# First attention of a four-layer stack: column sums in groups of four, turned scores issued earlier, the last softmax moved ahead of band products

## The reference

```python
def _L0_attn_ref(x, w_qkv, w_out, pos_bias, scale_embed, if_gain):
    _OFFSETS = list(range(41)) + [128, 48, 192]
    qkv = x @ w_qkv
    q, k, v = jnp.split(qkv, 3, axis=-1)        # then (B, H, T, HD)
    idx = jnp.arange(T)[:, None] - deltas[None, :]
    valid = idx >= 0
    k_g = k[:, :, idxc]
    v_g = v[:, :, idxc]
    k_mod = k_g * (1.0 + scale_embed)
    scores = jnp.einsum('bhtd,bhtjd->bhtj', q, k_mod) * scale
    scores = scores + pos_bias.T[None, :, None, :]
    scores = jnp.where(valid[None, None], scores, jnp.finfo(scores.dtype).min)
    attn = jax.nn.softmax(scores, axis=-1)
    out = jnp.einsum('bhtj,bhtjd->bhtd', attn, v_g)
    out = out * if_gain[None, :, None, None]
    return out @ w_out

x = x + 0.5 * _L0_ffn_ref(_layernorm(x), ...)
x = x + _L0_attn_ref(_layernorm(x), ...)
x = x + 0.5 * _L0_ffn_ref(_layernorm(x), ...)
```

## Time and profile before

| | |
|---|---|
| median of three runs | 3477.29 us (3476.79 to 3479.61) |
| the profiled execution, its own time | 3482.6 us |
| its span | 3480.8 us |
| busy: PE, DVE, ACT, POOL | 89%, 70%, 52%, 25% |
| the attention stage's products, first to last sum | 121.7 to 363.5 us |
| last `close` of the stage (L787) | 429.5 us |

### The profile page before, as it was taken

One profiled execution on the slowest core, in us unless ns is written; L12 is line 12 of the kernel. 1 busy time (PEld: TensorE's weight loads), 2 busy tenths in 40 slices (PEclk: granted clock), 3 DMA queues, 4 the chain that ended last, 5 costly groups with the idle time before them and its releaser, 6 DMA issues. The chain is left out here.

```text
span 3480.8 us, 62786 instructions
## 1 busy us (share of the span) xinstructions
PE 3111.7 (89%) x24941; PEld 1708.0 (49%) x24941; DVE 2437.7 (70%) x5433; ACT 1804.4 (52%) x3292; POOL 857.5 (25%) x801
## 2 busy tenths in 40 slices
PE   4899868999799999999798979888998899898899
PEld 3455745666522222222465557566776223332677
DVE  8877388778599999994877854645335888883433
ACT  2222236777467777777577753133222366677221
POOL 0324109677200000000867720001302111212000
PEclk9899979999879999999999989898999599998899
DMA  1044403111150000000311110001101400000100
GB/s 53 14 123 120 98 9 83 27 35 31 44 187 1 2 1 1 2 1 1 80 29 35 32 35 1 2 27 49 49 1 58 124 2 30 34 2 1 47 1 13
DMA packets 77882, 129.26 MB, mean 37 GB/s; under 512 B 12772, under 2 KB 52616, under 8 KB 77384
## 3 DMA queue, kind: packets, MB, share of 16 engines
q1 hardware_dynamic: 77592, 125.25, 12.7%
HBM read 77.39 MB, written 34.19 MB: 32 GB/s over the span
## 5 line engine op out<-in xcount | busy, mean ns | idle before, releaser
L2008 ACT ACTIVATE AR<-ps 128x1024 f32<-128x1024 f32 (+2 forms) x756 | 717.6, 995 | 289.4 <-PE ps L1909 220.8
L2091 DVE TENSOR_REDUCE AR<-ps 128x1 f32<-128x512 f32 x1296 | 809.2, 683 | 48.1 <-PE ps L1878 47.1
L1909 PE MATMUL ps<-AR 32*128 32x512 bf16 (+3 forms) x4992 | 537.9, 378 | 9.3 <-ACT AR L2008 5.6
L1878 PE MATMUL ps<-AR 32*128 32x512 bf16 (+3 forms) x1664 | 478.3, 397 | 43.8 <-DVE AR L2091 13.4
L1926 PE MATMUL ps<-AR 128*32 128x512 f32 (+3 forms) x3328 | 439.1, 601 | 4.3 <-ACT AR L2013 3.9
L2500 PEld LDWEIGHTS ps<-AR 128*128 128x128 f32 x3072 | 362.9, 192 | 60.5 <-issue 47.5
L1878 PEld LDWEIGHTS ps<-AR 32*128 32x128 bf16 x1664 | 119.7, 92 | 551.1 <-DVE AR L2091 411.1
L2659 DVE SCALAR_TENSOR_TENSOR X<-ps,AR,X 128x128 f32<-128x128 f32 x512 | 143.7, 344 | 345.7 <-PE ps L2500 345.3
L2500 PE MATMUL ps<-AR 128*128 128x128 f32 x3072 | 363.1, 275 | 0.0
L2475 PE MATMUL ps<-XT,AR 128*128 128x512 f32 x672 | 307.7, 594 | 0.0
L1909 PEld LDWEIGHTS ps<-AR 32*128 32x128 bf16 x4992 | 185.1, 94 | 152.8 <-ACT AR L2008 48.2
(11 more groups left out here) (326 smaller groups left out, 5150.5 us busy)
## 6 DMA issues: line engine op xcount, KB each, us to landing
AR<-AR SPq DMA_DIRECT2D x124, 128.0 KB, 2.3
band<-AR SPq DMA_DIRECT2D x32, 450.0 KB, 4.7
AR<-band SPq DMA_DIRECT2D x32, 448.0 KB, 5.0
AR<-in_c_rot SPq DMA_DIRECT2D x64, 128.0 KB, 2.2
AR<-in_L3f_w SPq DMA_DIRECT2D x30, 256.0 KB, 5.7
rows_KA<-AR SPq DMA_DIRECT2D x32, 128.0 KB, 2.4
AR<-scr_bias SPq DMA_DIRECT2D x32, 128.0 KB, 3.2
AR<-in_L2f_w SPq DMA_DIRECT2D x30, 128.0 KB, 2.7
```

The lines of the kernel that those rows point to most:

```text
L1878: e.matmul(g.bank[b][:, 0:w], QA[rows, q, 128 * i:128 * i + 128], KA[rows, q, 512 * first:512 * first + w], start=way != "kept", stop=True ...
L1909: t = e.matmul(g.bank[h][:, lo:512], K[32 * h:32 * h + 32, q, 128 * kt:128 * kt + 128], Q[32 * h:32 * h + 32, q, queries], start=y == 0, s ...
L2008: e.activation(dst[:, :, lo:512], src[:, :, lo:512], ACT.Exp, scale=self.scale).then_inc(*s.up("exp" if u else "left", k, i, *((1,) if u e ...
L2091: e.tensor_reduce(o, g.bank[b][:, 0:w], AXX, ALU.max).then_inc(*s.up("reduced", k, n, h, st, kc))
```

## The change

`scores` gives each step its place itself. Where the plan before had one `gather` between two products, four products behind, it now has four gathers in a row after every fourth product, the last of the four being two products behind. `lift` is split: `raise` is PE's part (L634), placed ahead of DVE's part, which keeps the name. For the first three chunks it stands at the place of the `exp` of the tile before. In the last chunk the lift, exp and norm steps of the four tiles stand close together, ahead of most band products of the third chunk (tiles 10 and 11), and every `through` of the last chunk stands ahead of the next tile's first turn. The `close` of chunk 2 moves to directly behind the third chunk's last tile and takes the statistics of the next stage's chunks 0 to 2 with it. In `sync` the loads 12 to 14 move behind the store of the next tile, and POOL's three first roots move ahead. The same work is done as before.

```diff
--- before.py
+++ after.py
@@ -471,7 +471,7 @@
 
 
 
-    SCORE_LAG, NPR, FAR, ROW, KEYS = 4, 11, (41, 43), 1800, 112
+    NPR, FAR, ROW, KEYS = 11, (41, 43), 1800, 112
 
     def allocate(self, g):
         ar = g.ar
@@ -502,29 +502,31 @@
         self.WO = ar.f32(4, 128)
         at = []
         for c in range(4):
-            at += [(c + (i + 0.5) / (2 * NJ), x) for i, x in enumerate(self.scores(c))]
+            at += self.scores(c)
             at += [(0.1 + 0.1 * b, ("project", 0, 0, b)) for b in range(8) if not c]
             for i in range(4):
-                soft = c + 1.02 + 0.15 * i
-                at += [(soft, ("lift", c, i, 4 * c + i)), (soft + 0.05, ("exp", c, i, 4 * c + i)),
-                       (soft + 0.12, ("norm", c, i, 4 * c + i))]
-                far = soft + 0.67
-                at += [(far + 0.02 * y, ("turn", c, y, 4 * c + i)) for y in range(4)]
-                at += [(far + 0.1, ("value", c, i, 4 * c + i)), (far + 0.13, ("taken", c, i, 4 * c + i)),
-                       (far + 0.16, ("through", c, i, 4 * c + i))]
-            at += [(far + (0.36 if c == 2 else 0.18), ("close", c, 0, 0))]
+                n = 4 * c + i
+                soft = c + 1.04 + 0.15 * i if c < 3 else 4.03 + 0.03 * i
+                norm = soft + (0.12 if c < 3 else 0.04)
+                at += [(soft - (0.09 if i and c < 3 else 0.02), ("raise", c, i, n)), (soft, ("lift", c, i, n)),
+                       (soft + (0.05 if c < 3 else 0.01), ("exp", c, i, n)), (norm, ("norm", c, i, n))]
+                far = soft + 0.67 if c < 3 else 4.3 + 0.2 * i
+                at += [(far + 0.02 * y, ("turn", c, y, n)) for y in range(4)]
+                at += [(far + 0.1, ("value", c, i, n)), (far + 0.13, ("taken", c, i, n)), (far + 0.16, ("through", c, i, n))]
+            at += [(far + 0.18, ("close", c, 0, 0))]
         self.plan = [x for _, x in sorted(at, key=lambda y: y[0])]
 
     def scores(self, c):
+
         js = []
         for gr in range(6):
             js += [j for j in [8 * gr + x for x in (0, 2, 4, 6, 1, 3, 5, 7)] if j < NJ]
         out = []
-        for i in range(NJ + self.SCORE_LAG):
+        for i in range(NJ + 2):
             if i < NJ:
-                out.append(("product", c, js[i], NJ * c + i))
-            if i >= self.SCORE_LAG:
-                out.append(("gather", c, js[i - self.SCORE_LAG], NJ * c + i - self.SCORE_LAG))
+                out.append((c + (i + 0.5) / NJ, ("product", c, js[i], NJ * c + i)))
+            if i % 4 == 1 and i > 4:
+                out += [(c + min(i + 0.5, NJ - 0.1) / NJ, ("gather", c, js[y], NJ * c + y)) for y in range(i - 5, i - 1)]
         return out
 
     def by_pool(self, n):
@@ -552,14 +554,12 @@
         wo = I["L0_attn_w_out"].rearrange("(g a d) n -> a d g n", g=4, a=4, d=8)
         for a in range(4):
             e.dma_start(self.WO[32 * a:32 * a + 8, :, :], wo[a]).then_inc(*s.up("d_w2", k, a, by=16))
-        for x in range(14):
+        for x in range(16):
             self.store(e, s, x)
-            if x < 13:
+            if x < 12:
                 self.load(e, s, x)
-        self.load(e, s, 13)
-        self.store(e, s, 14)
-        self.store(e, s, 15)
-        self.load(e, s, 14)
+            if x > 12:
+                self.load(e, s, x - 1)
         self.load(e, s, 15)
 
     def store(self, e, s, x):
@@ -620,7 +620,7 @@
                     e.wait_ge(*s.at("s8", k, *((c, gr - 2) if gr > 1 else (c - 1, gr + 4))))
                 e.matmul(g.bank[b][p:p + 32, :], self.W2[:, j, :], self.PR[n % self.NPR], start=j % 2 == 0,
                          stop=j % 2 == 1, skip_group_check=True).then_inc(*s.up("gathered", k, n))
-            if what == "lift":
+            if what == "raise":
                 if j == 0:
                     e.wait_ge(*s.at("s8", k, c, 5))
                 if n:
@@ -780,13 +780,11 @@
                                 ALU.mult).then_inc(*s.up("weighted", k, n, "run"))
                 e.tensor_tensor(to[:, :, 48], self.SM[:, j, :, 42], self.sm[:, j, :], ALU.mult).then_inc(*s.up("weighted", k, n))
             if what == "close":
-                for i in range(3) if c == 3 else ():
-                    settle(e, s, g, k + 1, i)
                 xs = g.X[:, 4 * c:4 * c + 4, :].rearrange("p a b -> p (a b)")
                 e.wait_ge(*s.at("through", k, 4 * c + 3))
                 e.tensor_tensor(xs, g.bank[7], xs, ALU.add).then_inc(*s.up("added", k, c))
-                if c == 3:
-                    settle(e, s, g, k + 1, 3)
+                for i in range(3) if c == 2 else (3,) if c == 3 else ():
+                    settle(e, s, g, k + 1, i)
 
     def gpsimd(self, e, s):
         g, k = self.g, self.k
@@ -832,8 +830,10 @@
                 e.tensor_tensor(self.UF, far, bc(self.WF[:, n % 4, 1, :], [128, 16, 8], 2), ALU.mult).then_inc(*s.up("unit", k, n, 1))
                 e.wait_ge(*s.at("unit", k, n, 1))
                 e.tensor_tensor(to, to, self.UF, ALU.add).then_inc(*s.up("paired", k, n))
-        for c in range(4):
-            root(e, s, g, k + 1, c)
+            if what == "value" and n == 13:
+                for i in range(3):
+                    root(e, s, g, k + 1, i)
+        root(e, s, g, k + 1, 3)
 
 
 class Timetable:
```

## The result

| | before | after |
|---|---|---|
| median of the runs on the same chip | 3478.45 us (3476.79 to 3483.91, 4 runs) | 3456.2 us (3452.05 to 3457.85, 4 runs) |
| ratio to before, 95% | 1 | 0.9932 [0.9914, 0.9949] |
| the profiled execution, its own time | 3482.6 us | 3454.95 us |
| its span | 3480.8 us | 3453.2 us |
| first product of the stage, last `close` | 121.75, 429.54 us | 120.79, 409.42 us |

The change saves 22.3 us by the medians, 0.7%. The forecast was 3460 (3445 to 3472), faster by over 0.2%.

A forecast was written before the change was run, and what follows sets the result against it. The stage was taken to alternate: DVE sets the pace in chunk 0 and each later chunk's first half, PE in the second half and tail. Terms 5 - 6.1 - 9.7 - 10.1 + 0.5 + 3 = -17.4 gave 3460 us (3445 to 3472).

The forecast's parts named there:

- Chunk 0, +5: First chunk: DVE waits longer for V projections standing directly behind a group of sums; +5 us, bounds 0 and 8.
- Chunk 1, -6.1: First lift to lift of tile 4: 58.4 us in place of 64.5, with 16 products' sums in four blocks.
- Chunks 2 and 3, -9.7 and -10.1: Lone sums between turns merge: 61.4 us for 71.15 and 60.4 for 70.5, including DVE waits of 2.7 and 1.5.
- The tail, +0.5: Lift of tile 12 to last close: 61.7 us against 61.2, as the new order adds waits; bounds -3 and +6.
- the clock, +3: Granted clock falls behind PE waits at three places, tail and middle of chunks 2 and 3; 3 us together, 0 to 8.
- the 4.4 us wait: In the tail PE stands 4.4 us at tile 10's projection, its values' copy queued on ACT behind three exponentials.
- The sum, -17.4: Whole kernel: 5 - 6.1 - 9.7 - 10.1 + 0.5 + 3 = -17.4 us, giving 3460 us.
- Waits at tiles 4, 8 and 12: Sign of being right: DVE's waits for PE's turned scores at these tiles fall to about 8 to 12 us.
- The busy time of L621 near 70 us: Sign of being right: PE's busy time for the sums falls from 116 us towards 70.
- Groups that give it back: Rival, 8%: groups stop PE until their last product, keeping chunks 2 and 3 at 70 us; kernel 3477.
- The slower case: Rival, 6%: repeated waits keep the tail's clock at its lower level, last five tiles +34 us; kernel 3491.
- Fuller overlap: Rival, 6%: DVE's waits vanish, chunks 2 and 3 take about 51 us each, not 61; kernel 3440.

The follow-up runs named there:

- e1: Kernel before with the groups of four sums alone, turned scores directly ahead of the lift, last chunk in its old order: 3474.25 us, ratio 0.9983.
- e6: Changed kernel with the eight V projections of chunk 0 placed just ahead of a group of sums instead of behind it: 3446.45 us, ratio 0.9907.
- e8: Changed kernel with V projections ahead of groups, last chunk's output projections behind the next first turn, second tile's exponential earlier, closes of chunks 0 and 1 later: 3439.33 us.
- e4: Kernel before with the last chunk's new order, close, loads and roots alone: 3477.96 us, ratio 0.9994.
- e9: Changed kernel with band products of the first three chunks 0.50 instead of 0.67 of a chunk behind their softmax: 3466.84 us, ratio 0.9963.

## Why the prediction was right

The time lies in the range and the mechanism holds, with one reservation that e1 shows (chunks 2 and 3 below). Three sums were loose: the waits listed for chunk 0 add up to 5.8 rather than 5, and six tiles of band products at the prices given are 39.6 us rather than 40.2, and the upper bounds reach 21.3 us rather than 22. None changes the forecast by more than 1 us.

**Chunk 0, +5.** Measured +4.3, which is just the change in these waits (5.60 less 1.32). The waits of L745 are as named: 1.94 at the start (1.32 before), 1.02 at projection 3, 1.62 at 5 (forecast 1.5) and 1.02 at 6 (1.0); those expected at 4 and 7 did not come. e6 shows that they are the cause, and that the term could have been had at less than nothing.

**Chunk 1, -6.1.** Measured -5.0. The granted clock was 0.83 in this chunk against 0.92 before: turned scores at 166.37 us took 5.52, as they had before the change, and those at 187.43 did so again, behind waits of 2.16 and 0.73 us for products. The second fall is new (5.45 us from start to start in place of 2.97) and is more than the missing 1.1 us; how much of it reached the end of the chunk was not separated. The clock's price stood in a term of its own, but that term had expected falls in chunks 2 and 3 and not here.

**Chunks 2 and 3, -9.7 and -10.1.** Measured -10.0 and -10.3. The steps hold one by one: waits of 2.34 and 1.53 us for the exponential and the `close` where 2.7 and 1.5 were worked out, lone sums that merge at 1.0 for a block. One block of each chunk costs 1.82 instead of 1.0, which the sum had missed. What the words ahead of it left out is that the merging gives this only together with the earlier turned scores: the sum used both (it let no lift inside a chunk wait), the sentence named one. e1 alone is 5.1 us in chunk 3.

**The tail, +0.5, and the clock, +3.** The tail measured +1.9. A tile takes 8.31 us (8.2 forecast), with the waits of 0.72 at each:

```profile
383.29 1.16 PE L677 MATMUL ps<-AR 128*128 128x128 f32 x8 [0.72 <-ACT AR L710]
...
391.60 1.16 PE L677 MATMUL ps<-AR 128*128 128x128 f32 x8 [0.72 <-ACT AR L710]
```

The wait for the copy of tile 10's values is 1.11 us, not 4.4, because PE came late to it:

```profile
356.69 5.51 PE L634 MATMUL ps<-C,AR 128*128 128x64 f32 x24 [0.99 <-DVE AR L756]
362.13 2.07 PE L658 MATMUL ps<-C,AR 128*128 128x128 f32 x8
364.13 1.94 PE L665 MATMUL ps<-AR 112*32 112x64 f32 x64
...
368.40 1.16 PE L677 MATMUL ps<-AR 128*128 128x128 f32 x8 [1.11 <-ACT AR L710]
```

The wait of 0.99 us for the lift of tile 14 was forecast (1.2), and the clock fell behind it. The three slow pieces cost 4.3 us over 2.94, 1.16 and 1.10, and took the place of 3.3 us of waiting. The forecast placed the fall behind the 4.4 us wait; it came one step earlier and took the place of most of it, so both terms were right only in their sum. Inside chunks 2 and 3, where two more falls were expected, the clock was 1.00. That the clock term fits is luck: of its three places one had a fall, and the other fall came in chunk 1.

**The sum, -17.4.** The stretches give -19.2 with the clock in them. By the median -22.3: 5 us more than forecast, inside the range. The part beyond the stage was forecast at nothing and is not a result of the change that any row shows; it is within the 3024 to 3047 us that those stages took.

**The signs.** Waits at tiles 4, 8 and 12 between 8 and 12 us: right. The busy time of L621 near 70 us: wrong. By the view that the 116 comes from it is 105.1 (115.9 before), but that view adds up the records that read XN and those that read AR, and in a merged block these run at the same time. By the windows, which count such time once, it fell from 107.8 to 82.8 us, and in chunks 2 and 3 from 56.2 to 35.6. In chunk 0 and in the first half of each chunk PE waits for single products inside a group, and the sums still go one by one, at 1.04 for two records. The groups merge only where PE is behind, which is also only where it counts.

**The rivals.** Groups that give it back are refuted by chunks 2 and 3 at 61.1 and 60.2 us; in e1, without the earlier turned scores, they did give half of it back. The slower case, a clock that stays low in the tail, did not come: the last four tiles, with two waits of about 0.7 us each and 8.31 us from one to the next, ran at full speed (clock 1.00 from 376 to 409 us). The swing that the Trainium skill warns of (TensorE: Matmul & The Clock Gate, A second HAM failure mode: psum-queue depth-cycling) is not in these rows. Fuller overlap has its direction in e8 (58.8 and 57.9), far from 51.

## What to carry to other kernels

When two engines take turns at setting the pace inside one loop, a change that takes work off one of them pays only if the other isn't made to wait in its own half; test such parts together as well as alone, since 8 and 2 us became 18 here (5.1 and 0.0 became 9.4 in the one chunk where all had the full clock). Before a small difference is put down to an order of steps, compare PE's busy time for the same records: e4's 1.5 us went away with it. Sums of 32 columns should be issued so that every block holds all four column groups, and what needs an engine's early answer should stand ahead of a block, not behind it. Where a wait and a slow stretch of the clock lie in a row on one path, forecast them as one item: the second hides the first.

## What was not expected of the hardware

- A wait of 0.99 us on TensorE was enough to be followed by turned scores of 5.51 us in place of 2.94, and values of 2.07 in place of 1.16, while pairs of waits of 0.7 us in every tile of 8.31 us left the pace whole. In the kernel before, the same wait (0.98 us at 389.13) was followed by turned scores of 3.30 us, and only the turns behind them were slow (3.35 in place of 1.91). In e4 a wait of 3.81 us at 389.53 was followed by turns at full speed, with the clock at 1.00 over the whole tail. And in e9 the same pair of waits for products (2.2 and 0.7 us) was followed by 5.52 us of turned scores in chunks 1 and 3 and by 3.04 in chunk 2. The slow stretches read here all stood behind a wait, but the wait alone does not tell whether one comes.
- A lone sum in one column group costs the same passes as four in four groups (1.0 us), and four in two groups 1.84: the switch between forms of 32 and 128 columns is hidden or at most 0.1 us.
